# Cross-attention and FFN in eight groups on one core: a separate instruction order for the first group's body, new orders for the others, ScalarE's block transfers in pairs

## What is computed

```python
x = x + xattn(layernorm(x), ctx)       # one head, 512 wide
x = x + ffn(layernorm(x))
# xattn: q = LN(m1) Wq + bq; k, v from LN(ctx); softmax(q k^T / sqrt(512)) v; @ Wo + bo
# ffn:   h = bitlinear(x, w_fc) + gate * (x v^T fast_b^T u^T)     # hidden 2048, rank 16
#        bitlinear(relu(h)^2, w_proj)     # ternary weights, scaled by row
```

## Time and profile before

| | |
|---|---|
| median of 3 runs | 805.66 us (803.67 to 807.49) |
| the profiled execution | 805.04 us, its span 803.0 us |
| granted TensorE clock | 0.999 |
| busy | PE 97%, PE's weight loads 80%, DVE 68%, ACT 47%, POOL 19% |
| HBM | 27.64 MB read, 8.39 MB written |

### The profile page before, as it was taken

One profiled execution on the slowest core, in us unless ns is written; L12 is line 12 of the kernel. 1 busy time (PEld: TensorE's weight loads), 2 busy tenths in 40 slices (PEclk: granted clock), 3 DMA queues, 4 the chain that ended last, 5 costly groups with the idle time before them and its releaser, 6 DMA issues.

```text
span 803.0 us, 10829 instructions
## 1 busy us (share of the span) xinstructions
PE 777.0 (97%) x3877; PEld 642.9 (80%) x3877; DVE 543.3 (68%) x1100; ACT 374.9 (47%) x705; POOL 150.0 (19%) x171
## 2 busy tenths in 40 slices
PE   6999988999999999999999999999999999999998
PEld 4678767887888778887888788887888788888886
DVE  5998857667757685577766685577766686476434
ACT  5997545335551644326542554326542554424332
POOL 3241130112202022022201122012301122012001
PEclk9999999999999999999999999999999999999999
DMA  9753141034410551134410452124420441021001
GB/s 314 273 144 102 17 77 56 36 54 69 127 40 1 85 112 53 40 46 69 118 57 1 70 86 94 40 36 74 98 83 0 70 75 55 0 35 45 27 0 53
DMA packets 180554, 56.93 MB, mean 71 GB/s; under 512 B 167666, under 2 KB 168068, under 8 KB 180500
## 3 DMA queue, kind: packets, MB, share of 16 engines
q1 hardware_dynamic: 150368, 51.51, 26.2%
q10 hardware_dynamic: 30132, 4.73, 3.4%
HBM read 27.64 MB, written 8.39 MB: 45 GB/s over the span
## 4 chain that ended last, share of the span: by engine, by line
PE 77%; SPq 6%; DVE 5%; ACT 3%; ACTq 3%; DMA 3%; issue 2%; DVEq 0%
PE G L1183 23%; PE O L1299 22%; PE H L1318 22%; SPq L505 5%; ACTq L788 3%; PE H L1324 3%; DVE rbuf L1074 2%; DMA Wv_s<-in_L_xattn_Wv_dram 2%; ACT rbuf L749 1%; PE H L1167 1%; PE G L1265 1%; PE O L1372 1%; DMA n_blocks<-n_rows 1%; PE H L1183 1%; ACT qbuf L757 1%
## 5 line engine op out<-in xcount | busy, mean ns | idle before, releaser
L1299 PE MATMUL O<-projT,qbuf 128*128 128x512 f32 x992 | 246.9, 391 | 6.7 <-DVE qbuf L1078 6.7
L1299 PEld LDWEIGHTS O<-projT,qbuf 128*128 128x128 f32 x992 | 184.1, 188 | 47.7 <-DVE qbuf L1078 10.6
L757 ACT ACTIVATE qbuf<-rbuf 128x512 fp32r<-128x512 f32 x125 | 79.1, 633 | 148.5 <-DVE rbuf L1074 112.1
L1074 DVE TENSOR_TENSOR rbuf<-rbuf 128x512 f32<-128x512 f32 x128 | 95.5, 746 | 61.9 <-ACT rbuf L749 61.8
L1318 PE MATMUL H<-even_group,fcT 128*128 128x512 f32 x512 | 127.8, 392 | 2.9 <-ACT rbuf L749 2.9
L1318 PE MATMUL H<-odd_group,fcT 128*128 128x512 f32 x512 | 127.3, 391 | 0.0
L749 ACT ACTIVATE rbuf<-H,scf 128x512 f32<-128x512 f32 x128 | 86.9, 679 | 68.2 <-PE H L1324 63.2
L1318 PEld LDWEIGHTS H<-even_group,fcT 128*128 128x128 f32 x512 | 94.9, 188 | 22.4 <-ACT rbuf L749 3.3
L1078 DVE TENSOR_TENSOR qbuf<-rbuf,qbuf 128x512 fp32r<-128x512 f32 x125 | 88.8, 710 | 33.7 <-ACT qbuf L757 30.9
L1318 PEld LDWEIGHTS H<-odd_group,fcT 128*128 128x128 f32 x512 | 95.3, 188 | 19.3
L1183 PE MATMUL G<-Wvo,tT 128*128 128x512 f32 x270 | 65.6, 391 | 0.0
(11 more groups left out here) (196 smaller groups left out, 1066.9 us busy)
## 6 DMA issues: line engine op xcount, KB each, us to landing
xb<-in_x_dram SPq DMA_DIRECT2D x8, 1024.0 KB, 4.8
n_blocks<-n_rows SPq DMA_DIRECT2D x112, 64.0 KB, 2.3
ctxb<-in_ctx_dram SPq DMA_DIRECT2D x8, 768.0 KB, 4.3
n_blocks<-ctxb SPq DMA_DIRECT2D x112, 48.0 KB, 2.1
wring<-in_L_ffn_w_fc_dram SPq DMA_DIRECT2D x16, 256.0 KB, 5.3
wring<-in_L_ffn_w_proj_dram SPq DMA_DIRECT2D x16, 256.0 KB, 3.1
out_dram<-x2a SPq DMA_DIRECT2D x8, 512.0 KB, 3.0
x_blocks<-x_rows SPq DMA_DIRECT2D x56, 64.0 KB, 3.0
```

Source lines behind the costliest of these rows:

```text
L757: nc.scalar.activation(squares(b, j)[:, HI, :], rbuf[:, j % 2, :], ACT.Copy).then_inc(sqhi_made, 1)
L1074: nc.vector.tensor_tensor(rbuf[:, j % 2, :], rbuf[:, j % 2, :], rbuf[:, j % 2, :], ALU.mult).then_inc(square_made, 1)
L1299: mm = pe.matmul(banks[f"O{t}"][:, :], qbuf[:, j % 2, h, t * P:(t + 1) * P], projT[:, j, :], start=(j == 0 and h == HI), stop=(j == NFF - ...
```

## The change

The lists of all four engines are laid anew. Body 0 has lists of its own (`FIRST_ORDER`), which leave out what the prologue has run. `xmove2`, `xmove3` with four DMAs each become `xmove4` to `xmove7` with two each. `store(6, 0)` becomes `store(NG - 2, 0)`, which is the same. Nothing is added to or taken from what is computed.

```diff
--- before.py
+++ after.py
@@ -115,29 +115,53 @@
 
 BODY_ORDER = {
     "pe": (
-        "down-:14 L:0 down-:15 up:0 up:1 up:2 down:0 up:3 down:1 up:4 down:2 up:5 t:0 t:1 t:2 down:3 s:0 up:6 s:1 s:2 "
-        "down:4 pT:0 up:7 s:3 down:5 pT:1 up:8 down:6 w:0 w:1 up:9 w:2 down:7 a:0 a:1 up:10 a:2 down:8 a:3 up:11 "
-        "down:9 up:12 down:10 up:13 down:11 up:14 down:12 up:15 down:13 "
+        "down-:14 L:0 down-:15 up:0 up:1 up:2 up:3 down:0 down:1 up:4 up:5 t:0 t:1 down:2 t:2 down:3 s:0 up:6 s:1 s:2 "
+        "up:7 pT:0 down:4 s:3 up:8 down:5 pT:1 down:6 w:0 w:1 up:9 w:2 down:7 a:0 a:1 a:2 down:8 up:10 a:3 up:11 "
+        "down:9 up:12 up:13 down:10 up:14 down:11 down:12 up:15 down:13 "
     ).split(),
     "act": (
-        "L:0 up:0 hi:0 up:1 hi:1 n1hi0 up:2 n1hi1 hi:2 n1hi2 up:3 n1hi3 hi:3 up:4 n2hi0 n2hi1 t:0 n2hi2 hi:4 t:1 up:5 "
-        "t:2 hi:5 s:0 n2:0 up:6 s:1 n2:1 s:2 n2:2 pT:0 n2:3 s:3 hi:6 pT:1 up:7 hi:7 up:8 w:0 hi:8 w:1 w:2 up:9 hi:9 "
-        "up:10 hi:10 up:11 hi:11 xmove2 nx0+ up:12 hi:12 xmove3 nx1+ up:13 nx2+ hi:13 nx3+ nc0+ xhi0 up:14 nc1+ xhi1 hi:14 xhi2 "
-        "up:15 nc2+ xhi3 hi:15 nc3+ "
+        "L:0 up:0 hi:0 n1hi0 up:1 up:2 n1hi1 hi:1 up:3 n1hi2 hi:2 hi:3 n1hi3 n2hi0 up:4 n2hi1 t:0 n2hi2 t:1 up:5 t:2 "
+        "hi:4 n2:0 s:0 n2:1 up:6 s:1 s:2 n2:2 hi:5 up:7 pT:0 n2:3 hi:6 s:3 up:8 pT:1 hi:7 w:0 hi:8 w:1 w:2 up:9 hi:9 "
+        "up:10 hi:10 nx0+ nx1+ up:11 hi:11 xmove4 up:12 xmove5 xmove6 xmove7 hi:12 up:13 nx2+ nx3+ up:14 hi:13 nc0+ "
+        "xhi0 xhi1 nc1+ hi:14 xhi2 xhi3 up:15 hi:15 nc2+ nc3+ "
     ).split(),
     "dve": (
-        "L:0 out01 out23 n1raw0 sq:0 lo:0 n1raw1 sq:1 lo:1 n1raw2 sq:2 n1lo0 lo:2 n1lo1 n1raw3 n1lo2 sq:3 n1lo3 lo:3 "
-        "n2raw0 n2raw1 n2lo0 t:0 n2raw2 sq:4 n2lo1 n2lo2 lo:4 t:1 t:2 sq:5 s:0 n2:0 s:1 lo:5 n2:1 s:2 sq:6 n2:2 pT:0 "
-        "n2:3 s:3 xs01+ lo:6 sq:7 pT:1 lo:7 sq:8 w:0 w:1 xs23+ w:2 lo:8 a:0 a:1 sq:9 nX0 lo:9 sq:10 nX1 a:2 lo:10 a:3 "
-        "nX2 sq:11 nX3 lo:11 cs01+ sq:12 cs23+ lo:12 sq:13 xraw0 xraw1 lo:13 xraw2 sq:14 xlo0 xraw3 lo:14 xlo1 xlo2 "
-        "sq:15 xlo3 lo:15 "
+        "L:0 n1raw0 out01 sq:0 out23 lo:0 n1raw1 sq:1 n1lo0 n1lo1 lo:1 n1raw2 sq:2 n1raw3 lo:2 sq:3 n1lo2 n2raw0 "
+        "n1lo3 n2raw1 t:0 n2lo0 lo:3 n2raw2 sq:4 t:1 n2lo1 n2lo2 t:2 lo:4 n2:0 s:0 sq:5 n2:1 sq:6 s:1 s:2 n2:2 lo:5 "
+        "pT:0 s:3 n2:3 lo:6 xs01+ pT:1 sq:7 sq:8 lo:7 w:0 w:1 xs23+ w:2 sq:9 lo:8 a:0 a:1 a:2 nX0 nX1 nX2 lo:9 sq:10 "
+        "a:3 lo:10 sq:11 nX3 lo:11 cs01+ sq:12 cs23+ lo:12 sq:13 xraw0 xraw1 xraw2 lo:13 sq:14 xraw3 xlo0 lo:14 xlo1 "
+        "xlo2 sq:15 xlo3 lo:15 "
     ).split(),
     "pool": (
-        "out23 residual xs23+ a:0 a:1 a:2 a:3 cs23+ "
+        "out23 residual a:0 a:1 a:2 xs23+ a:3 cs23+ "
     ).split(),
 }
 
 
+FIRST_ORDER = {
+    "pe": (
+        "down:0 down:1 up:3 up:4 up:5 down:2 t:0 t:1 up:6 t:2 down:3 s:0 s:1 down:4 s:2 up:7 pT:0 s:3 down:5 up:8 "
+        "pT:1 down:6 w:0 w:1 up:9 down:7 w:2 up:10 a:0 a:1 down:8 a:2 up:11 a:3 down:9 down:10 up:12 down:11 up:13 "
+        "up:14 down:12 down:13 up:15 "
+    ).split(),
+    "act": (
+        "up:2 n1hi0 hi:2 n1hi1 up:3 hi:3 n1hi2 n1hi3 t:0 up:4 n2hi0 t:1 n2hi1 up:5 n2hi2 hi:4 t:2 n2:0 hi:5 up:6 s:0 "
+        "s:1 n2:1 n2:2 s:2 pT:0 hi:6 up:7 n2:3 s:3 pT:1 w:0 up:8 hi:7 w:1 hi:8 w:2 up:9 up:10 hi:9 hi:10 up:11 nx0+ "
+        "hi:11 xmove4 xmove5 xmove6 xmove7 up:12 up:13 hi:12 nx1+ nx2+ nx3+ hi:13 up:14 xhi0 xhi1 nc0+ xhi2 hi:14 "
+        "xhi3 nc1+ nc2+ up:15 nc3+ hi:15 "
+    ).split(),
+    "dve": (
+        "sq:2 n1raw0 n1raw1 n1raw2 lo:2 n1lo0 sq:3 n1lo1 n1raw3 n1lo2 n1lo3 t:0 lo:3 n2raw0 n2raw1 sq:4 n2raw2 n2lo0 "
+        "n2lo1 t:1 t:2 n2lo2 sq:5 lo:4 s:0 n2:0 s:1 lo:5 n2:1 s:2 sq:6 n2:2 pT:0 s:3 sq:7 lo:6 n2:3 xs01+ pT:1 lo:7 "
+        "sq:8 w:0 xs23+ w:1 w:2 lo:8 sq:9 lo:9 a:0 sq:10 a:1 a:2 lo:10 sq:11 nX0 a:3 nX1 nX2 nX3 cs01+ lo:11 sq:12 "
+        "cs23+ sq:13 lo:12 xraw0 xraw1 lo:13 xraw2 sq:14 xraw3 xlo0 lo:14 xlo1 xlo2 sq:15 xlo3 lo:15 "
+    ).split(),
+    "pool": (
+        "residual a:0 a:1 xs23+ a:2 a:3 cs23+ "
+    ).split(),
+}
+
+
 def step(word):
 
     kind, _, n = word.partition(":")
@@ -147,9 +171,8 @@
 def body_steps(b, engine):
 
     if b < GROUPS - 1:
-        skipped = [word for word in BODY_ORDER[engine] if word[-1] == "+" and b == GROUPS - 2
-                   or word.startswith(("down-", "out")) and b == 0]
-        return [step(word) for word in BODY_ORDER[engine] if word not in skipped]
+        words = BODY_ORDER[engine] if b > 0 else FIRST_ORDER[engine]
+        return [step(word) for word in words if not (word[-1] == "+" and b == GROUPS - 2)]
     out = [("down-", NFF - 2), ("L", 0), ("down-", NFF - 1), "out01", "out23"]
     for j in range(FIRST_LATE):
         out += [("up", j), ("sq", j), ("hi", j)]
@@ -434,8 +457,7 @@
             early = prologue_steps(engine)
             for b, st in early:
                 steps(b, [st])
-            steps(0, [st for st in body_steps(0, engine) if (0, st) not in early])
-            for b in range(1, NG):
+            for b in range(NG):
                 steps(b, body_steps(b, engine))
 
         block = stack.enter_context(nc.Block())
@@ -570,7 +592,7 @@
                 move_blocks(x_blocks, x_rows, x_moved, range(2))
                 if b + 2 < NG:
                     move_n1(b + 2)
-            store(6, 0)
+            store(NG - 2, 0)
             for t in range(3):
                 sp.wait_ge(y_added, 4 * (NG - 1) + t + 1)
                 sp.dma_start(out_v[NG - 1, t // 2][:, t % 2 * D:(t % 2 + 1) * D], x2[1][:, t, :]).then_inc(stored, 16)
@@ -781,11 +803,11 @@
                         act.wait_ge(xraw_made, KD * b + k + 1)
                         nc.scalar.activation(halves[:, HI, k, :], raw[:, LO, k, :], ACT.Copy).then_inc(xhi_made, 1)
                     elif kind[:5] == "xmove":
-                        i = int(kind[5])
+                        n = int(kind[5])
                         act.wait_ge(xn_made, 4 * (b + 2))
                         act.wait_ge(unit_full, n_full(b, ("s", 3)))
-                        for q in range(4):
-                            act.dma_start(*block_of(x_blocks, x_rows, i, q)).then_inc(x_moved, 16)
+                        for q in (2 * (n % 2), 2 * (n % 2) + 1):
+                            act.dma_start(*block_of(x_blocks, x_rows, n // 2, q)).then_inc(x_moved, 16)
                     elif kind[:2] == "nc":
                         t, g = int(kind[2]), b + 1 + (kind[-1] == "+")
                         if t == 0:
```

## The result

The changed kernel takes 806.53 us (median of 20 runs, 804.29 to 807.62) against 805.14 us for the kernel before (20 runs beside it): a ratio of 1.0014, 95% interval 1.0008 to 1.0021. Forecast were 799.5 us and a gain of 0.7%. The profiled execution took 804.62 us, its span 802.7, on the low side of its runs.

A forecast was written before the change was run, and what follows sets the result against it. PE was taken to bound the kernel, other engines mattering only through its waits. Gains of 3.0 (body 0) and 5.6 (bodies 1 to 6) less 2.7 for a new wait gave 5.9 us off, forecast 799.5 us, range 796 to 805.

The forecast's parts named there:

- What bounds, and the ceiling: Whole kernel: PE bounds, a wait-free body lasts 89.90 us; order alone gives at most 5.6 + 6.6 = 12.2 us.
- Body 0, front: Start of body 0: waits of 2.87 and 2.15 us go, smaller ones come; gain 3.0 us.
- Body 0, end: End of body 0: new waits of 1.8 us in all against 1.6 before, so no gain.
- ACT's eight transfers: End of body 0: eight block DMAs ahead of `up:12` take some 5.7 us, making `up:14` 0.3 us late.
- less up to 1 if the eight DMAs take longer: Body 0: reservation that its 3.0 us gain could shrink by up to 1 us.
- Bodies 1 to 6, end: Boundaries of bodies: waits there go; that and what follows can give back all 5.6 us.
- Bodies 1 to 6, front: Start of each body: late `n1raw0` and four POOL collisions make `down:1` wait, 0.45 us a body, 2.7 us in all.
- With little to spare: Start of bodies 1 to 6: `up:3` was taken as covered, needing ACT's `up:1` at 11.6 against 11.7.
- the landing at 6.3 to 6.6 us: Start of bodies 1 to 6: n1 blocks land so `n1raw0` starts about 6.3 us in, 6.6 if slower.
- a sign against it: Bodies 1 to 6: windows not 90.2 to 90.5 us, above all `n1raw0` later than 7 us, would mean prediction wrong.
- the second rival: Start of bodies 1 to 6: new wait 1.0 to 1.4 us a body, 7.2 instead of 2.7, so 804 us; chance 0.22.
- The rule weighed on the transfers: Block DMAs: skill calls issue time usually small; trace had ACT blocked 0.66 us each, though page made pairs worth nothing.

The follow-up runs named there:

- g3: Changed kernel with `lo:1` moved ahead of `n1lo0` and `n1lo1` in VectorE's list: 803.63 us, ratio 0.9989 to the kernel before.
- g2: Changed kernel with `out01`, `out23` ahead of `n1raw0`, and ACT's transfers of bodies 1 to 6 in fours again: 797.23 us, ratio 0.9909 to the kernel before.
- g1: Changed kernel with evacuation first, operations reordered so PE depends less on the blocks' landing, and body 0's end laid anew: 795.93 us, ratio 0.9894 to the kernel before.
- e2: Kernel before with the new lists for bodies 1 to 6 alone, body 0 keeping its old list: 809.04 us, ratio 1.0052 to the kernel before.
- f1: Changed kernel with `sq:0` put back behind `out23` and `n1raw0` left at the head of VectorE's list: 811.64 us, ratio 1.0082 to the kernel before.

## Why the prediction was wrong

**What bounds, and the ceiling.** Right in kind: only PE's waits counted. The wait-free body was taken as 89.90 us from body 6 of before; six wait-free bodies take 538.29 us, 89.7 each. There was 6.5 us to be had in bodies 1 to 6 (544.8 - 538.3), not 5.6.

**Body 0, front.** Right: waits of 0.59, 0.97 and 0.44 us at `down:1`, `up:5` and `s:0` were forecast with 0.8, 1.3 and 0.5 in distances of starts and measured with 0.86, 1.13 and 0.61. `s:0` stands 26.5 us behind `down:0`; forecast was 26.3 (127.6 - 101.28).

**Body 0, end.** The mis-sized term is ACT's eight transfers: 5.7 us from the four of rows 7, measured 6.65. The first four took 3.03 us, the second four 3.61, up to 0.96 each. SP was issuing beside all of them, as beside the four of rows 7, so that alone does not explain it, and why the later ones take longer stays open. PE's `up:14` was 1.6 us late instead of 0.3. The wait at `down:12` (forecast 1.5, measured 1.20 of idle, 1.4 in starts) came out near the forecast only because `lo:12` and PE were both over 1 us later than in the sum. Body 0 gained 1.5 us and not 3.0; "less up to 1 if the eight DMAs take longer" was named and not taken into the sum.

**Bodies 1 to 6, end.** Right: no wait at a boundary is left. Which of the edits brought it was not tried one by one, but for the pairs, which did not.

**Bodies 1 to 6, front.** This is the step that failed, in its size: the mechanism was as written (the evacuation behind `n1raw0`, four additions of POOL that each shut out one VectorE operation or are shut out), and it cost 545.8 - 538.3 = 7.5 us, 1.25 a body, where 0.45 was taken. Three errors of the sum, all in the same direction:
- It took the latest of `up:3` and `down:1` as the one wait. They are two: `up:3` waits for ACT's `up:1` (0.14 to 0.77 us in distances of starts), which delays all of PE, and still `down:1` waits 0.66 us, since with `n1raw0` later both chains move. "With little to spare" for `up:3` was read as nothing lost.
- It took the landing at 6.3 to 6.6 us (its own 544.6 + 12.43 - 550.9 gives 6.1). It was 6.5 to 7.2 in the profiled execution, 6.8 on average: SP issued the first transfer 5.7 to 5.9 us before the body instead of 6.3, and the 16 took 12.43 to 12.93. Over 7 us, which the prediction named as a sign against it, it was in bodies 2 and 5; bodies 2 and 3 of `g3` had 8.0. In the kernel before, the evacuation in front had hidden most of this.
- Each of the two waits costs some 0.3 us more than its idle time, half before and half behind the restart. Bodies 1 to 6 have 4.5 us of idle (545.77 - 541.27), and the other 3 us of the 7.5 are PE's longer steps around the waits. The sum, which worked in starts, left out what comes behind.

Of the 0.8 us a body between 0.45 and 1.25, the landing accounts for some 0.4 (6.8 against the 6.45 between its two values), an estimate from these rows; the two other points are the rest.

The case that came is the second rival, "the new wait is 1.0 to 1.4 us a body": 804 us, with a chance of 0.22. The other executions are later still than the profiled one (median 806.53 against 804.62). That this is the spread of the landing is argued from `g3` and from the six bodies of the profiled execution, not shown run by run.

**The rule weighed on the transfers.** The Trainium skill (DMA: Bandwidth & Descriptors, Issuing engines are not separate DMA queues) has the issue time as usually small beside the transfer. `g2` agrees that the grouping is worth nothing where ACT has slack; the eight in a row of body 0 cost 6.65 us of ACT, which is not small.

**The numbers.** 805.04 - 1.5 (body 0) - 6.5 (the waits of bodies 1 to 5) + 7.5 (the new waits) gives 804.5; the profiled execution took 804.62. These terms are read from the two profiles, so the sum says only that next to nothing changed outside bodies 0 to 6.

## What to carry to other kernels

In an engine's own order, an operation that waits for a transfer belongs behind everything that is ready and that others wait for; where it leads, the transfer's spread becomes the time of the engine that bounds. The evacuations (one input in PSUM, one in SBUF) ran beside POOL's additions at full speed here, 1.28 us for two, and the operations with two SBUF inputs did not, so let POOL's work start while VectorE does the former. VectorE's busy time does not tell what that is worth: it is 552.5 us in the changed kernel and 553.8 in the fastest (`g1`). When several chains in a body have little slack and all hang on one start, sum what each loses once the start is late: they pay one after another.

## What the runs showed of the hardware

- VectorE's operations with two SBUF inputs and POOL's additions exclude each other, one whole instruction at a time, in either order: `n1lo0`, issued just as an addition got in, took 1.78 us instead of 0.65 (the run of two, 2.38), and VectorE was busy 9.2 us more in the changed kernel with the same 1100 instructions. With additions of one column `sq:0` is back at 0.68 and the two `n1lo` at 1.28.
- Sixteen transfers of 64 KB issued by SP took 10.70 us to issue and 12.43 to land at best; 12.13 and 13.86 at worst, in the same kernel. ACT's eight in a row took 6.65 us, four of them 2.88.
- TensorE's granted clock fell to 0.5 (1.2 GHz) during or behind some waits of PE and not others: for 6.83 us during one of 2.83 (`e2`), for 3.41 us behind waits of 1.87 and 2.05 (`f1`), and not behind those of 1.20 to 1.63 us in `f1` nor, in the profile of the kernel before, at the one of 2.87.
- A short wait cost PE about 0.3 us beyond its idle time: 892 ns from start to start where 227 is usual and 504 were shown as idle, and then 0.14 us in the eight matmuls behind it (changed kernel, 293.30).
